# Second attention of a transformer kernel: softmax sums of two of four head groups from key halves that GpSimd adds

## The reference

```python
q = jnp.einsum('bsc,hcd->bhsd', xn, wq)      # 16 heads of 32 channels
k = jnp.einsum('btc,hcd->bhtd', yn, wk)
v = jnp.einsum('btc,hcd->bhtd', yn, wv)
a = jax.nn.softmax(jnp.einsum('bhsd,bhtd->bhst', q, k) * D ** (-0.5), axis=-1)
if causal:
    mask = (jnp.arange(t)[None, :] > jnp.arange(s)[:, None]).astype(a.dtype)
    a = a * mask
o = jnp.einsum('bhst,bhtd->bhsd', a, v)
x_out = x + o @ li1_w + li1_b
```

## Time and profile before

| | value |
|---|---|
| median of 3 runs | 1420.15 us |
| span of the profiled execution | 1416.2 us |
| what lies around the span (median less span) | 3.95 us |
| mean granted TensorE clock | 0.981 of full |
| PE busy | 1327.3 us, 94% |
| DVE busy | 978.6 us, 69% |
| ACT busy | 854.1 us, 60% |
| POOL busy | 662.4 us, 47% |
| second attention, about | 622 to 956 us of the span |

### The profile page before, as it was taken

The page is one execution under the profiler, slowest core; times in us unless marked ns, Lnnn a source line. Parts: engine busy times, 40 slices in busy tenths (PEclk is TensorE's granted clock), DMA queues, the critical chain, the costliest instruction groups (busy, mean ns, idle before and its releaser), DMA issues.

```text
span 1416.2 us, 43090 instructions
## 1 busy us (share of the span) xinstructions
PE 1327.3 (94%) x17982; PEld 862.9 (61%) x17982; DVE 978.6 (69%) x2228; ACT 854.1 (60%) x1349; POOL 662.4 (47%) x1134
## 2 busy tenths in 40 slices
PE   8899999998999999899999999997989999999895
PEld 4455555554455554456777777665767677677585
DVE  6688887876555554577888888754568887876243
ACT  3577777775666655657777777654456566532352
POOL 4456555543100002235666666452347776455265
PEclk9999999997999999999999999999999999999898
DMA  7000000000320000000001001102001111122451
GB/s 227 3 3 3 3 3 3 3 3 2 102 70 1 1 0 1 1 2 18 32 18 33 32 18 33 33 32 61 1 25 43 44 48 54 39 90 85 136 168 46
DMA packets 55186, 53.78 MB, mean 38 GB/s; under 512 B 9305, under 2 KB 49245, under 8 KB 54738
## 3 DMA queue, kind: packets, MB, share of 16 engines
q1 hardware_dynamic: 51090, 44.20, 10.2%
q0 software_dynamic: 2816, 6.11, 1.2%
q10 hardware_dynamic: 1088, 0.72, 0.3%
HBM read 20.34 MB, written 14.49 MB: 25 GB/s over the span
## 4 chain that ended last, share of the span: by engine, by line
PE 75%; DVE 8%; ACT 4%; POOL 4%; DMA 3%; SPq 3%; issue 2%; POOLq 0%; ACTq 0%; DVEq 0%
PE psum L1561 6%; PE psum L1589 4%; PE psum L949 4%; PE psum L1223 4%; PE psum L950 4%; PE psum L951 4%; PE psum L1187 3%; DVE a_nm L611 3%; PE psum L2612 3%; SPq L803 2%; DMA a_QT<-a_nmT 2%; PE psum L529 2%; PE psum L1532 2%; PE psum L2049 2%; PE psum L1573 2%
## 5 line engine op out<-in xcount | busy, mean ns | idle before, releaser
L1644 DVE TENSOR_REDUCE b_nm<-psum 128x4 f16<-128x1024 f32 x128 | 156.5, 1223 | 52.1 <-PE psum L1566 51.4
L728 ACT ACTIVATE a_prob<-psum 128x768 f32<-128x768 f32 (+1 forms) x160 | 136.1, 853 | 64.0 <-PE psum L466 62.3
L611 DVE TENSOR_REDUCE a_nm<-psum 128x4 f16<-128x1024 f32 (+1 forms) x96 | 117.2, 1222 | 44.0 <-PE psum L496 31.0
L780 POOL TENSOR_SCALAR_AFFINE_SELECT a_prob<-a_prob 128x512 f32<-128x512 f32 x128 | 81.8, 639 | 126.8 <-ACT a_prob L728 126.5
L171 POOL TENSOR_TENSOR f_ln_rstd<-f_ln_tmp,pow_half 128x4 f32<-128x4 f32 x24 | 25.4, 1058 | 201.0 <-DVE f_ln_tmp L160 201.0
L1077 ACT ACTIVATE xo_sb<-psum,f_w_h_s 128x512 f32<-128x512 f32 x64 | 44.0, 688 | 88.3 <-PE psum L951 88.3
L1561 PE MATMUL psum<-b_QTh,b_KTh 32*128 32x256 f16 x512 | 70.4, 272 | 7.0 <-DVE b_nm L1644 5.2
L1566 PE MATMUL psum<-b_KTh,b_QTh 32*128 32x256 f16 x512 | 70.9, 274 | 0.0
L1566 PE MATMUL psum<-b_KTl,b_QTh 32*128 32x256 f16 x512 | 69.6, 269 | 0.0
L1566 PE MATMUL psum<-b_KTh,b_QTl 32*128 32x256 f16 x512 | 69.6, 269 | 0.0
L1561 PE MATMUL psum<-b_QTh,b_KTl 32*128 32x256 f16 x512 | 69.3, 268 | 0.0
(11 more groups left out here) (457 smaller groups left out, 4651.3 us busy)
## 6 DMA issues: line engine op xcount, KB each, us to landing
f_h_wh<-b_rden SPq DMA_DIRECT2D x64, 128.0 KB, 2.1
f_h_wh<-c_rden SPq DMA_DIRECT2D x64, 128.0 KB, 2.1
expert_in<-empty SPq DMA_DIRECT2D x8, 662.5 KB, 11.2
m_xt<-expert_in SPq DMA_DIRECT2D x7, 662.5 KB, 5.8
m_w<-in_L_ffn_w_dram SPq DMA_DIRECT2D x16, 256.0 KB, 2.6
x_sb<-in_x_dram SPq DMA_DIRECT2D x8, 256.0 KB, 4.7
f_w_h_w<-in_L_ffn_h_w_dram SPq DMA_DIRECT2D x2, 1024.0 KB, 7.4
out_dram<-m_send SPq DMA_DIRECT2D x8, 256.0 KB, 2.5
```

Source lines behind the costliest of these rows:

```text
L611: nc.vector.tensor_reduce(out, psum[:, banks, :].rearrange("p i (a b) -> p i a b", a=groups), X, ALU.max, negate=True).then_inc(max_done, 1)
L728: nc.scalar.activation(prob[unit % 5][:, :, 0:width], psum[:, first:first + 2, 0:width], ACT.Exp, scale=SCALE).then_inc(exp_done, 1)
L780: nc.gpsimd.affine_select(out=diagonal, in_=diagonal, compare_op=ALU.is_ge, fill=0.0, base=0, pattern=[[0, 4], [1, P]], channel_multiplier ...
L1644: v.tensor_reduce(self.nm[:, :, :].rearrange("p t (j r) -> p j t r", r=32)[:, 2 * e:2 * e + 2, :, g], self.pr.psum[:, 2:4, :].rearrange("p ...
```

## The change

For the even groups (g = 0 and 2) GpSimd adds the two key blocks of the probabilities of each unit, right behind the unit's selections, into one of four new tiles `both` [128, 2, 256]. `tensor_sums` of these groups then takes one product per head from `both`, 4 products in place of 8, and waits for two additions of the group (`halves_added`). The odd groups stay as they were.

```diff
+        self.both = [sb(f"both{i}", [P, 2, T]) for i in range(4)]
...
-        for kb in range(2):
+        if g % 2 == 0:
+            t.wait_ge(self.halves_added, 4 * n + g + 2)
             for j in range(4):
                 inst = t.matmul(self.pr.psum[D * j:D * j + D, 6, 0:T], self.group_col[:, g, :],
-                                self.prob[(unit + j // 2) % 4][:, j % 2, kb * T:kb * T + T], start=(g == 0 and kb == 0),
-                                stop=(g == self.G - 1 and kb == 1), skip_group_check=True)
+                                self.both[(g + j // 2) % 4][:, j % 2, :], start=(g == 0), stop=False, skip_group_check=True)
+        else:
+            for kb in range(2):
+                for j in range(4):
+                    inst = t.matmul(self.pr.psum[D * j:D * j + D, 6, 0:T], self.group_col[:, g, :],
+                                    self.prob[(unit + j // 2) % 4][:, j % 2, kb * T:kb * T + T], start=False,
+                                    stop=(g == self.G - 1 and kb == 1), skip_group_check=True)
         inst.then_inc(self.sums_done, 1)
...
+    def gpsimd_added(self, unit):
+
+        g, (n, u) = self.nc.gpsimd, divmod(unit, self.U)
+        group, prob = u // 2, self.prob[unit % 4]
+        if n:
+            g.wait_ge(self.sums_done, self.G * (n - 1) + group + 1)
+        g.tensor_tensor(self.both[(group + u % 2) % 4][:, :, :], prob[:, :, 0:T], prob[:, :, T:2 * T],
+                        ALU.add).then_inc(self.halves_added, 1)
...
             self.gpsimd_select(s)
+            if s // 2 % 2 == 0:
+                self.gpsimd_added(s)
```

More of the change, by code:

```diff
@@ L1418, in __init__ @@
         self.sums_done, self.av_done, self.num_out = sem("sums_done"), sem("av"), sem("num")
-        self.sums_out = sem("sums_out")
+        self.sums_out, self.halves_added = sem("sums_out"), sem("halves_added")
         self.rden_done, self.rb_there, self.oT_ready = sem("rden"), sem("rb"), sem("oT")
```

## The result

The changed kernel takes 1434.1 us (median of 7 runs, 1427.5 to 1437.7), the one before 1419.9 (7 runs, 1415.9 to 1426.3). The two medians are 1.0100 apart; the ratio on record, by which all kernels here are compared, is 1.0089, 95% interval 1.0061 to 1.0117. That is slower, and outside the range given. The profiled execution has a span of 1432.4 us and a time of 1434.1; the span of before was 1416.2.

What follows compares the result with a forecast made beforehand. TensorE was taken to bound a batch (21.01 of 21.10 us), ScalarE pacing slot 7. Terms −1.9 (steady batches), −1.8 and −0.4 (early and late batches), +3.6 (end) made −0.5: 1419.6 us, 8-in-10 range 1415.5 to 1427.5.

Steps and rivals of the forecast that it cites:

- Additions of 1.24 us, pushes of 1.18: On GpSimd, each 128x512 addition takes 1.24 us and delays what stands behind it in the queue by 1.18.
- the rival's threshold of 1.35: GpSimd becoming the bound (chance 0.23) decides once an addition takes 1.35 us, by its own length or through VectorE.
- Slot 3 wins 0.17 a batch: Sums of g = 0, batches 2 to 12: 0.27 won after a 0.17 wait, less 0.10, leaves 0.17 a batch.
- The 0.10 taken for slot 0: VectorE's L1679 meets GpSimd's L1796 and starts late, delaying unit 0's pair and both slot 3 additions by 0.1 us.
- Slots 4 to 7, where g = 2 "neither wins nor loses": TensorE waits 0.55 for additions before the sums in slot 7, saves 0.44; ScalarE's pace covers the rest; net zero.
- Batches 0 and 1 win 0.9: In batches 0 and 1 L1679 doesn't run, so g = 0 wins its full 0.44 in each; −0.9 for these batches.
- Batches 13 and 14, and g = 2 of 13: Without layer norm work on GpSimd, g = 0 wins 0.44 in each batch, and g = 2 of batch 13 wins 0.4.
- The end costs 3.6: In batch 15 TensorE waits for GpSimd's additions; values of g = 2 come 3.64 later, and +3.6 us stays in the span.
- rival C: From the experiments, no chance given: the cost is TensorE's wait for the additions in front of the sums.
- rival B: From the experiments, no chance given: GpSimd's queue is longer, so its selections, powers and low halves come late.
- Rival "GpSimd becomes the bound": Additions delay the sums of slots 3 and 7 and the end; at 1.45 us each +9.3, 1429.4 us; chance 0.23.
- What would show it: Signs: period 20.8 to 21.0, TensorE wait about 0.5 at g = 2, end 3 us later; above 21.2 wrong, slow side.

Runs made afterwards that it cites:

- e6: Changed kernel with additions and short sums for g = 0 alone, in batches 0 to 14; ratio 0.9975 to the kernel before, period 20.98 us.
- e2: Changed kernel without additions or the wait for them; even groups' sums take key block 0 alone; ratio 0.9949 to the kernel before, period 20.74 us.
- e7: Changed kernel with additions and short sums for g = 2 alone, in batches 0 to 14; ratio 1.0042 to the kernel before, period 21.91 us.
- e3: Changed kernel with a 128x6 GpSimd power for each addition, still waited for; even sums take key block 0 alone; 1429.4 us, ratio 1.0066 to the kernel before.
- e1: Changed kernel with the same 64 additions read by nobody; all sums take 8 products without waiting; ratio 1.0085 to the kernel before, period 21.91 us.
- e12: Kernel before plus one unread addition a batch (unit 4), made behind the first two powers of slot 4, none in batch 15; ratio 1.0006, period 21.10 us.

## Why the prediction was wrong, point by point

- *Additions of 1.24 us, pushes of 1.18*: 1.27 and 1.28, pushes of 1.24 and 1.22. Right in the main; the rival's threshold of 1.35 by their own length was not reached.
- *Slot 3 wins 0.17 a batch*: 0.13 in the changed kernel, 0.12 in e6. The size is right, its terms less so, and that is partly luck. The removal is worth 0.37 there (e2) and not 0.44, and the wait is 0.24 and not 0.17; 0.37 − 0.24 = 0.13. The 0.10 taken for slot 0 didn't come: the pair of unit 0 starts 1.10 behind the start of its exponential in both kernels.
- *Slots 4 to 7, where g = 2 "neither wins nor loses"*: the failed step. It moved GpSimd's queue and kept the old times for all else, so VectorE's L188 and the maximum behind it had no delay in the sum. The runs showed L188 held for 1.03 us and TensorE's block 0.80 later for it; the period of e7 is 0.81 longer. The loss is not in slot 7, where I looked for a TensorE wait of 0.55 put down to GpSimd, but in slot 5, at the block that waits for VectorE's maximum. I had seen that these engines keep each other out, and in both directions: the pair of 1.68 in the earlier trace rows, where GpSimd loses, and L1660 with 0.89 in the earlier trace rows, where VectorE does. But I carried it to L1679 alone, and priced it at 0.1. The sentence against the rival, that most of VectorE's work beside the additions reads PSUM, holds for most instructions and not for the one that counts. I never laid the new positions of the additions over VectorE's timeline, where L188 at 761.28 lies right under the addition that my own text puts at 782.37 − 21.10 = 761.27.
- *Batches 0 and 1 win 0.9*: they lost 1.5. L188 runs there too, and is held (1.21 at 654.96, in batch 1; 0.60 before). *Batches 13 and 14, and g = 2 of 13*: the 0.74 and 0.76 measured are near the 0.4 to 0.9 of the text, where the layer norm work is gone.
- *The end costs 3.6*: it cost 8.24, a second term of the sum that was mis-sized. The waits were forecast in kind (1.41 and the queue behind unit 5's pair), and came 2.04 and 3.35 long. From the start of batch 15 to the values of g = 2 it is 19.13 us in place of 12.90, +6.23 where 3.64 was forecast; from there to the last reciprocal, where nothing was forecast, 5.92 in place of 3.91. The projections are 1.26 and 1.34 slower, and the values of g = 2 too (0.43 for 8 products, 0.22 before), all at the lower clock. I had left the clock out. An estimate of its share from these rows is 1.26 for the first projection and 2.01 behind the values of g = 2, together 3.3 of the 4.6 that the forecast lacks. With powers in place of additions (e3) the distance from the next to last to the last reciprocal is 23.70, with additions 23.53, with dead additions (e1) 17.19, and before 15.33. So here rival C is what counts, 6.3 of 8.2 with what the clock adds to it, and not what VectorE loses. The other 1.9 is rival B: in e1 the values of g = 2 wait 2.09 us for a selection that stands behind an addition in GpSimd's queue, where they waited 0.22 before. The share of the clock was not measured apart.
- *Rival "GpSimd becomes the bound"*: it named "VectorE keeping it out" as a cause and 1429.4 as the time. Its sign was right, its mechanism the wrong way round: it has waits of TensorE for additions in slots 3 and 7, and these are 0.24 and 0, and the additions stay at 1.27 and 1.28: VectorE doesn't hold them up, they hold up VectorE.
- *What would show it*: a period above 21.2 was named as wrong on the slow side. It was 21.79.

The Trainium skill (SBUF — State Buffer, section "SBUF: two separate sides") says of the ports that both engines share that whoever starts first holds them for its whole instruction, and "the other fully blocks". The additions agree that it blocks to the end. The pair of L188 at 742.23 is, one by one,

```profile
742.23 1.37 DVE L188 TENSOR_SCALAR b_z<-u_sb,b_lnx_mv,b_lnx_rstd 128x128 f32<-128x128 f32 x1
743.52 0.34 DVE L188 TENSOR_SCALAR b_z<-u_sb,b_lnx_mv,b_lnx_rstd 128x128 f32<-128x128 f32 x1
```

so the first is held: it ends at 743.60, 0.08 behind the addition's end (742.24 + 1.28 = 743.52), and the second takes 0.34 as before. Its row starts 0.01 before the addition's, so who got the ports first can't be read from the starts. The prediction's sentence on the Trainium skill (GPSIMD Engine Reference, Key points) named VectorE instructions with two SBUF inputs alone; the section names those "in a 2-port perf mode" beside them. L188 reads one tensor and is held all the same; whether it runs in such a mode, no run here shows.

## What to carry to other kernels

When work is added to GpSimd, lay each new instruction over VectorE's timeline of the same moments, and ask of each VectorE instruction there whether it is of a kind that is held (the list is below) and what waits behind it: the price is that instruction's delay less its cover, and both stand in the profile of before. A sum of busy time, or of GpSimd's own queue, doesn't see it. The place in the queue is worth more than the amount of work: the same addition 1.5 us later was free. And a new wait of some us on TensorE can have a second price, in the clock.

## What the runs showed of the hardware

- Held by an addition of 128x512 (two SBUF inputs): the tensor-scalar instructions L160 (0.17 to 0.74) and L188 (0.60 to 1.63 for two), each up to the addition's end. Not held: maxima and low halves that read PSUM (1.23 at 732.67 and 0.68 at 733.81, both as before, under the addition of 733.22), the reciprocal (1.74 under the addition in e12) and the statistics L151 and L155 (0.48 at 736.44 and 0.25 at 736.95, under the addition of 736.68).
- In the kernel before, too, VectorE was held: L1660 (two SBUF inputs) takes 0.89 beside L1785 of GpSimd, and 0.42 in the changed kernel, where the second L1785 (L1801 there) takes 0.92 in place of 0.67 instead. Beside a selection of 128x256 the second L188 of b_zi takes 0.43, where the first takes 0.33.
- A power of GpSimd on 128x6, 1.32 us long, doesn't hold L188 up, though it starts with it; nor L160, which starts 0.44 behind the start of such a power (the rows are of e3):

```profile
754.63 0.17 DVE L160 TENSOR_SCALAR b_lnx_tmp<-b_lnx_mv 128x2 f32<-128x2 f32 x1
...
759.80 0.60 DVE L188 TENSOR_SCALAR b_z<-u_sb,b_lnx_mv,b_lnx_rstd 128x128 f32<-128x128 f32 x2
```
```profile
754.19 1.33 POOL L1784 TENSOR_TENSOR b_both<-f_hT0l,pow_half 128x6 f32<-128x6 f32 x1
...
759.81 1.32 POOL L1784 TENSOR_TENSOR b_both<-f_hT0h,pow_half 128x6 f32<-128x6 f32 x1
```

So what holds VectorE doesn't go by the length of GpSimd's instruction. This differs from what the Trainium skill says (SBUF — State Buffer, section "SBUF: two separate sides"), that the ports are held for the whole instruction; the measurement decides. The power differs from the addition both in its operation and in the elements it moves; which of the two decides, no run here tells.

- In the changed kernel TensorE waited 2.04 us (947.20 to 949.24), and over the 5 us from the end of the wait the granted clock was 0.66; over the 5 us from the end of the wait of 3.35 us it was 0.50. It isn't so behind each wait of this length: in e1 TensorE waited 2.09 us for a selection, and the clock stayed at 1.00 (windows in the columns of the earlier trace rows).

```profile
958.11 0.30 PE L1612 MATMUL psum<-f_hT0h,b_V 128*32 128x128 f32 x2 [2.09 <-POOL b_late L1777]
```
```profile
955.00:960.00 5.00, 2.91 (x51) 2.06 (x50) 2.64 (x5) 1.54 (x2) 5.00 (x8) 1.00 0.00 0
960.00:965.00 5.00, 4.07 (x55) 2.77 (x54) 3.96 (x7) 2.06 (x3) 3.16 (x6) 1.00 0.00 0
```
